# Two PSUM banks for score half tiles and four for the ring, in place of three and three

## The chip, the cores and the metric

One core of a Trainium2 chip (trn2) runs the whole program. The metric is the device time of one execution in microseconds. TensorE (PE in the rows) multiplies, VectorE (DVE) and ScalarE (ACT) read its products from PSUM, GpSimd (POOL) works between SBUF tiles, SyncE (SP) issues most transfers. PSUM has eight banks of 512 fp32 columns, numbered 0 to 7 here.

## The reference, cut to what matters

Two layers of attention over a context of 1601 rows and a feed-forward part, on a batch of 4 with 256 rows of width 512. The change lies in the attention of the second layer, which is grouped: 16 query heads share 4 heads of keys and values.

```python
hidden = jnp.concatenate([context, latents], axis=1)      # 1601 + 256 rows
q = (latents @ Wq.T).reshape(b, q_len, H, HD)             # H = 16, HD = 96
k = (hidden @ Wk.T).reshape(b, s_len, KV, HD)             # KV = 4
v = (hidden @ Wv.T).reshape(b, s_len, KV, HD)
...
scores = jnp.einsum('bkgqd,bksd->bkgqs', q, k) * scale
attn = jax.nn.softmax(scores.astype(jnp.float32), axis=-1).astype(q.dtype)
out = jnp.einsum('bkgqs,bksd->bkgqd', attn, v)
out = out.transpose(...)
return out @ Wo.T
```

After it comes a layer normalisation and a feed-forward part with a small mixture (`L1_ffn`).

## The kernel before, in words

Three functions run one after the other: `context_products` (the context's keys and values), `latent_attention_and_ffn` (the first layer and its feed-forward part), and `grouped_attention` (line 1194 on), the third stage, which takes from about 1012 us to the end. Only that one is touched.

**Segments and tiles.** The stage has S = 16 passes, one for each pair of batch element and key head. They are called segments 0 to 15 here. A segment has 1024 query columns (4 query heads by 256 rows) and 1857 keys in KT = 15 key tiles of 128 (the last of 65). Scores of one tile are 128 keys by 1024 columns, computed as two half tiles of 512 columns, one PSUM bank each. Each half tile of scores is the sum of three matmuls (lines 1502, 1503, 1504), since keys and queries are split in a high and a low part; the column maxima are subtracted through extra rows of the first one.

**What each half tile goes through.** ACT takes the exponential twice (function `probs`): line 1604 writes it rounded to `ph`, line 1607 again in full precision to `pf`. Both read the scores' bank, and it is free when the second is done (semaphore `exp_done`). POOL subtracts them to `pl` (line 1417, `plo`). TensorE then multiplies with the values in three matmuls (lines 1522, 1523, 1525), into two accumulating banks, one for each half, which stay in use for the whole segment. The third waits for POOL. Line 1607 waits for POOL's subtraction of two half tiles ago.

**The ring.** All other products of the stage share a ring of banks: `ring_item` writes product number n into bank `M0 + n % RB`, after DVE has read product n - RB (line 1426). They are, for each segment, 32 products for the maxima of the next segment (line 1435, read by DVE at line 1690), two products of 9 matmuls with the output weights (1458, read at 1698), and in segments 5, 9 and 13 those of the feed-forward part of the batch element that is complete (1466, 1472, 1477, 1480, 1483). `beside(s)` lists the order for TensorE and for DVE alike.

**The order on each engine.** For each tile, TensorE issues the scores of tile kt + 1 (half 0, a ring product, half 1, a ring product) and then the values of tile kt (half 0, a ring product, half 1, a ring product), lines 1542 to 1553; from tile 12 on no ring product stands beside the values. Segment 0 has no ring product for its first tiles, segment 15 none for maxima. At the end of a segment, the maxima are transposed (line 1488, into bank `M0`), and DVE writes them as extra rows (line 96), on which the next segment's first scores wait.

**What stands in ACT's queue besides.** After the exponentials of tile 0 of the next segment, ACT copies the two accumulating banks to `o` (1652) and sends the row sums to eight partitions (1611). Behind tile 2 it waits until DVE has inverted them (1720) and sends them to DRAM (1615); behind tile 3 it waits for that to land and spreads them over 96 partitions (1619); behind tiles 6, 7 and 9 stand the steps that stack the output (1623, 1628, 1635). DVE's inversion stands in its own list after six maxima. In segments 5, 9 and 13 DVE also runs `layernorm` (lines 63 to 88), with a ring product's reading at each `pause` and `between`.

**The banks.** Scores use banks 0 to SB - 1, a half tile with running number i in bank `i % SB`; the accumulators are banks OB and OB + 1; the ring is banks M0 to M0 + RB - 1. TensorE's wait before half tile i of the scores is for `exp_done` of half tile i - SB:

```python
                    if 2 * n + half >= SB:
                        pe.wait_ge(exp_done, 2 * n + half - SB + 1)
                    out = bank((2 * n + half) % SB)[0:m, :]
```

Of the kernel before, what the change touches and what calls it, by code (L numbers as in the profile page):

```python
# [100 lines left out]
def build(nc, A, out):  # L101
# [10 lines left out]
    with ExitStack() as ctx:  # L112
        def sb(name, shape, dt=F32):
            return ctx.enter_context(nc.sbuf_tensor(name, shape, dt))

        ident = sb("ident", [P, P])
        negid = sb("negid", [QT, QT])
        ps = ctx.enter_context(nc.psum_tensor("ps", [P, 8 * BANK], F32))
        ln = {n: sb(f"ln_{n}", s) for n, s in
              (("st", [P, TT, 6]), ("mv", [P, TT, 2]), ("v", [P, TT]), ("t", [P, TT]), ("u", [P, TT]), ("y", [P, TT]))}  # L120
        w1T = sb("w1T", [P, DC, D])
        home = [sb(f"home{i}", [P, n], F32R) for i, n in enumerate((NK + 1, 2 * GC, NK + 1))]
        with ExitStack() as early:
            def weight(name, cols, dt=F32R):
                return early.enter_context(nc.sbuf_tensor(name, [P, DC, cols], dt))

            wkvh, wkvl = weight("wkvh", WV + WK), weight("wkvl", WV + WK)
            wqh, wql = weight("wqh", H1 * HD1), weight("wql", H1 * HD1)
            w0T = weight("w0T", D, F32)
            small = {n: early.enter_context(nc.sbuf_tensor(n, shape, F32)) for n, shape in  # L130
                     (("bias0", [P, D]), ("wqd", [P, DC, LQ]), ("wqk", [LQ, H0, 3 * HD0]), ("wvu", [P, NG * 2, 2, HD0 + 1]),
                      ("cq", [LQ, T]))}
            context_products(nc, A, ident, negid, ps, ln, home, wkvh, wkvl, wqh, wql, w0T, w1T, *small.values(),
                             k_scr, v_scr, cst_scr, cv_scr, wo_scr)
            latent_attention_and_ffn(nc, A, ident, negid, ps, ln, home, wkvh, wkvl, wqh, wql, w0T, *small.values(),
                                     cst_scr, cv_scr, q_scr, k_scr, v_scr, x_scr)
        grouped_attention(nc, A, ident, negid, ps, ln, home, q_scr, k_scr, v_scr, x_scr, wo_scr, sum_scr, o_scr, w1T, out)
# [1056 lines left out]
def grouped_attention(nc, A, ident, negid, ps, ln, home, q_scr, k_scr, v_scr, x_scr, wo_scr, sum_scr, o_scr, w1T, out):  # L1194
# [16 lines left out]
    with ExitStack() as ctx:  # L1211
# [69 lines left out]
        bm_done, zp_done, d_mm, y_done, o_st = sem("bm_scaled"), sem("zp_ready"), sem("delta_product"), sem("y_ready"), \  # L1281
            sem("out_stored")
        block = ctx.enter_context(nc.Block())
        OB, M0, RB, SB = 3, 5, 3, 3

        def bank(i, n=BANK):
            return ps[:, i * BANK:i * BANK + n]
# [550 lines left out]
```

## Time and profile before

| | |
|---|---|
| median of 3 runs | 1970.17 us (1968.33 to 1972.54) |
| the profiled execution | 1970.21 us |
| its span, first to last instruction | 1968.4 us |
| TensorE busy with matmuls | 1880.0 us, 96% of the span |
| DVE, ACT, POOL busy | 1036.9, 906.6, 631.3 us |
| mean granted TensorE clock | 0.966 of full speed |
| third stage | about 1012.7 to 1968.4 us |

Around the span lie 1.8 us of the execution. A row of a timeline gives start and duration in us, the engine, the line, what it wrote and read with the shapes, and in brackets the idle time before it and what ended that. Matmuls are pipelined: one is shown for about 0.4 us, but the next starts 0.23 us after it, so the start of the next one tells more than the duration. PEld is the loading of the weights for a matmul, SPq and ACTq are transfers issued by SP and ACT.

### The profile page before, as it was taken

The page shows a single profiled execution, that of the slowest core. Times are in us where ns is not written, and L with a number is a line of the kernel's source. Part 1 is how long each engine was busy: PE and PEld are TensorE (multiplying, and loading weights), DVE is VectorE, ACT ScalarE, POOL GpSimd, SP SyncE. Part 2 cuts the span into 40 slices and gives each one's busy share as a digit, 9 for nine tenths or more (in the row PEclk, how much of TensorE's full clock was granted, in tenths as well). Part 3 has the DMA queues.
Part 4 walks back from the last instruction along what each step waited for, and adds up shares of the span by engine and source line. Part 5 has one row for each costly group of instructions (what it writes and reads, how often), then busy time and mean ns, then how long its engine had stood idle before and what let it go on. Part 6 is the DMA issues. An engine that isn't in the chain of part 4 may idle for free. (4 is left out here: it accounts for less than half of the span.)

```text
span 1968.4 us, 23187 instructions
## 1 busy us (share of the span) xinstructions
PE 1880.0 (96%) x8570; PEld 1334.5 (68%) x8570; DVE 1036.9 (53%) x1983; ACT 906.6 (46%) x1726; POOL 631.3 (32%) x504
## 2 busy tenths in 40 slices
PE   7999997999999999999899999999999999999997
PEld 6999894444466465555577777767776777767763
DVE  3564435667665665666525444564545455554414
ACT  2333331444344334434236666545655466645650
POOL 0000000000000000000027777757776577765760
PEclk9999995999999999999989999999999999999996
DMA  5978963000111020021177444435544145543101
GB/s 180 287 246 256 291 205 98 0 1 17 43 44 45 16 75 22 33 77 33 54 205 178 121 120 111 111 88 131 133 123 123 51 105 141 131 123 96 53 25 43
DMA packets 192950, 208.42 MB, mean 106 GB/s; under 512 B 87425, under 2 KB 157569, under 8 KB 192838
## 3 DMA queue, kind: packets, MB, share of 16 engines
q1 hardware_dynamic: 177124, 188.92, 33.7%
q10 hardware_dynamic: 15714, 18.03, 3.0%
q8 instruction: 68, 1.11, 0.2%
q14 instruction: 44, 0.36, 0.1%
HBM read 128.90 MB, written 77.94 MB: 105 GB/s over the span
## 5 line engine op out<-in xcount | busy, mean ns | idle before, releaser
L1417 POOL TENSOR_TENSOR pl<-pf,ph 128x512 fp32r<-128x512 f32 (+1 forms) x480 | 623.5, 1321 | 270.9 <-ACT pf L1607 270.3
L1604 ACT ACTIVATE ph<-ps 128x512 fp32r<-128x512 f32 (+1 forms) x480 | 288.1, 600 | 369.8 <-PE ps L1504 309.7
L1690 DVE TENSOR_REDUCE pm<-ps 128x1 f32<-128x464 f32 x480 | 299.8, 636 | 203.0 <-PE ps L1435 199.6
L1140 DVE TENSOR_REDUCE pm<-ps 128x1 f32<-128x400 f32 (+3 forms) x544 | 285.3, 572 | 90.8 <-PE ps L987 86.8
L1047 ACT ACTIVATE pr<-ps 128x512 f32<-128x512 f32 (+1 forms) x416 | 219.6, 600 | 196.0 <-PE ps L919 195.2
L1607 ACT ACTIVATE pf<-ps 128x512 f32<-128x512 f32 (+1 forms) x480 | 289.1, 602 | 3.3 <-POOL pl L1417 2.5
L1406 POOL MEMSET vh<- 128x30 f32 x1 | 0.2, 154 | 700.3 <-POOLq L684 700.3
L932 PE MATMUL ps<-pr,cv 128*64 128x512 f32 (+1 forms) x832 | 210.6, 622 | 0.0
L1522 PE MATMUL ps<-ph,vh 128*97 128x512 f32 (+1 forms) x480 | 191.4, 399 | 0.0
L1525 PE MATMUL ps<-pl,vh 128*97 128x512 f32 (+1 forms) x480 | 190.1, 396 | 1.1 <-POOL pl L1417 0.8
L1523 PE MATMUL ps<-ph,vl 128*97 128x512 f32 (+1 forms) x480 | 189.2, 394 | 0.0
L1435 PE MATMUL ps<-kh,qh 96*128 96x464 f32 x320 | 121.3, 379 | 7.7 <-DVE pm L1690 7.5
L1502 PE MATMUL ps<-qh,kh 104*128 104x512 f32 x300 | 122.2, 407 | 0.1
L932 PEld LDWEIGHTS ps<-pr,cv 128*64 128x64 f32 (+1 forms) x832 | 51.9, 139 | 86.8 <-issue 60.8
L1525 PEld LDWEIGHTS ps<-pl,vh 128*97 128x97 f32 (+1 forms) x480 | 78.0, 163 | 38.7 <-POOL pl L1417 6.2
L901 POOL MEMSET home<- 96x1 f32 x1 | 0.1, 96 | 304.5 <-POOLq L158 304.5
L987 PE MATMUL ps<-home,ast 96*128 96x400 f32 (+1 forms) x256 | 91.6, 420 | 6.1 <-DVE pm L1140 2.6
L1523 PEld LDWEIGHTS ps<-ph,vl 128*97 128x97 f32 (+1 forms) x480 | 78.8, 164 | 26.6
L1522 PEld LDWEIGHTS ps<-ph,vh 128*97 128x97 f32 (+1 forms) x480 | 78.4, 163 | 24.0 <-issue 0.2
L987 PE MATMUL ps<-cst,ast 96*128 96x400 f32 (+1 forms) x256 | 84.3, 386 | 5.7 <-DVE pm L1140 4.1
L987 PEld LDWEIGHTS ps<-home,ast 96*128 96x128 f32 x256 | 49.9, 209 | 57.7 <-DVE pm L1140 28.5
L987 PEld LDWEIGHTS ps<-cst,ast 96*128 96x128 f32 x256 | 45.7, 192 | 54.0 <-DVE pm L1140 33.3
(264 smaller groups left out, 3104.0 us busy)
## 6 DMA issues: line engine op xcount, KB each, us to landing
woT<-wo_turned SPq DMA_DIRECT2D x30, 768.0 KB, 6.0
v_scr<-vst SPq DMA_DIRECT2D x16, 1152.0 KB
cnat<-in_ctx_dram SPq DMA_DIRECT2D x16, 768.0 KB
q_scr<-qst SPq DMA_DIRECT2D x48, 256.0 KB, 2.5
vh<-v_scr SPq DMA_DIRECT2D x15, 672.0 KB
vl<-v_scr SPq DMA_DIRECT2D x15, 672.0 KB
home<-k_scr SPq DMA_DIRECT2D x14, 696.4 KB, 8.4
k_scr<-home SPq DMA_DIRECT2D x24, 384.0 KB, 7.8
```

The costliest lines, as they stand in the source:

```text
L932: mm = pe.matmul(bank(OB)[64 * half:64 * half + 64, :], cv[0:keys[kt], b % 2, kt, :], pr[0:keys[kt], n % NPR, half * BANK:(half + 1) * BAN ...
L987: mm = pe.matmul(out[:, 0:k], queries, keys_t, start=True, stop=True)
L1047: act.activation(pr[0:keys[kt], n % NPR, half * BANK:(half + 1) * BANK], bank((2 * n + half) % SB)[0:keys[kt], :], ACT.Exp, scale=S0).then ...
L1140: dve.reduce_max(pm[:, j, ch:ch + 1], src[:, 0:(cuts if s < S else next_cuts)[ch][1]], AX)\
L1417: pool.tensor_tensor(pl[0:m, n % 2, cols], pf[0:m, half, :], ph[0:m, n % 2, cols].bitcast(F32), ALU.subtract).then_inc(plo, 1)
L1502: pe.matmul(out, kh[s % 3][:, k0:k0 + m], qh[s % 3][:, cols], start=True, stop=False)
L1522: pe.matmul(out, vh[0:m, s % 2, kt, :], ph[0:m, n % 2, cols], start=(kt == 0), stop=False)
L1523: pe.matmul(out, vl[0:m, s % 2, kt, :], ph[0:m, n % 2, cols], start=False, stop=False)
L1525: mm = pe.matmul(out, vh[0:m, s % 2, kt, :], pl[0:m, n % 2, cols], start=False, stop=(kt == KT - 1))
L1604: act.activation(ph[0:keys[kt], n % 2, cols], src, ACT.Exp, scale=S1).then_inc(phi, 1)
L1607: act.activation(pf[0:keys[kt], half, :], src, ACT.Exp, scale=S1).then_inc(exp_done, 1)
L1690: ins = dve.reduce_max(pm[:, j, ch:ch + 1], at[:, 0:cuts[ch][1]], AX)
```

## The change

One line. The ring gets banks 4 to 7 (it had 5 to 7), the scores get banks 0 and 1 (they had 0 to 2), the accumulators move from banks 3 and 4 to banks 2 and 3. All waits follow from the four numbers: that of the scores (line 1499) counts `exp_done` back by two half tiles and not three, that of the ring (line 1426) counts `ring_done` back by four products and not three. ACT's source (line 1601), DVE's source (line 1674), the copies of the accumulators (line 1652) and the bank of the transposed maxima (lines 1488 and 1670) follow too.

```diff
         block = ctx.enter_context(nc.Block())
-        OB, M0, RB, SB = 3, 5, 3, 3
+        OB, M0, RB, SB = 2, 4, 4, 2
```

## Rows read from the trace of the kernel before

**Rows 1.** The page, busy time of each engine (share of the span, instructions)

```profile
PE 1880.0 (96%) x8570; PEld 1334.5 (68%) x8570; DVE 1036.9 (53%) x1983; ACT 906.6 (46%) x1726; POOL 631.3 (32%) x504
```

**Rows 2.** Waits from 890 us on: waiter, releaser, total us, times, longest us

```profile
...
ACT ph L1604 <- DVE sums_inverted L1720: 49.4, 13, 6.6
...
PE ps L1435 <- DVE pm L1690: 11.2, 12, 1.2
...
ACT ph L1604 <- DMA sum_scr<-sums_inverted: 10.2, 5, 2.5
...
```

**Rows 3.** Timeline of segment 2: ACT at tile 4, TensorE at tile 5, half 1

```profile
1133.77 0.32 ACTq L1619 DMA_DIRECT2D o_inverted<-sum_scr  x1
...
1135.64 0.61 ACT L1607 ACTIVATE pf<-ps 128x512 f32<-128x512 f32 x1
...
1135.93 0.40 PE L1502 MATMUL ps<-qh,kh 104*128 104x512 f32 x1
```

**Rows 4.** Timeline of segment 10: the same place, with its two transfers

```profile
1589.15 0.28 ACTq L1615 DMA_DIRECT2D sum_scr<-sums_inverted  x1
...
1593.70 0.32 ACTq L1619 DMA_DIRECT2D o_inverted<-sum_scr  x1
...
1594.62 0.59 ACT L1607 ACTIVATE pf<-ps 128x512 f32<-128x512 f32 x1
...
1595.26 0.50 PE L1502 MATMUL ps<-qh,kh 104*128 104x512 f32 x1
...
1595.58 0.62 ACT L1607 ACTIVATE pf<-ps 128x512 f32<-128x512 f32 x1
...
1595.60 0.40 PE L1503 MATMUL ps<-qh,home 96*128 96x512 f32 x1
...
1595.84 0.39 PE L1504 MATMUL ps<-home,kh 96*128 96x512 f32 x1
...
1597.41 0.40 PE L1523 MATMUL ps<-ph,vl 128*97 128x512 f32 x1
...
1597.88 0.47 PE L1525 MATMUL ps<-pl,vh 128*97 128x512 f32 x1
```

**Rows 5.** Timeline of segment 5: TensorE, DVE and ACT at tiles 2 to 4

```profile
1287.18 0.48 PE L1435 MATMUL ps<-home 96*128 96x464 f32 x1 [1.10 <-DVE pm L1690]
...
1292.59 0.94 DVE L1720 RECIPROCAL sums_inverted<-sums 8x128 f32<-8x128 f32 x1
...
1293.83 2.81 DVE L1690 TENSOR_REDUCE pm<-ps 128x1 f32<-128x464 f32 x5
...
1294.50 0.48 PE L1435 MATMUL ps<-home 96*128 96x464 f32 x1 [1.16 <-DVE pm L1690]
...
1295.40 0.61 ACT L1607 ACTIVATE pf<-ps 128x512 f32<-128x512 f32 x1
...
1296.63 0.40 PE L1502 MATMUL ps<-qh,kh 104*128 104x512 f32 x1
```

**Rows 6.** Start of the stage: timeline, then two windows with PEclk, the granted clock

```profile
1016.46 0.59 ACT L1607 ACTIVATE pf<-ps 128x512 f32<-128x512 f32 x1
...
1017.10 0.79 PE L1502 MATMUL ps<-home 104*128 104x512 f32 x1 [0.21 <-ACT pf L1607]
...
1017.69 0.63 PE L1503 MATMUL ps<-home 96*128 96x512 f32 x1
...
1012.70:1022.10 9.40, 9.18 (x21) 6.43 (x22) 3.90 (x5) 4.22 (x8) 6.32 (x8) 0.50 0.94 213
1022.10:1032.00 9.90, 9.90 (x45) 7.58 (x44) 2.63 (x5) 6.41 (x13) 7.90 (x7) 0.99 1.05 303
```

**Rows 7.** Timeline of segment 15: half 1 of tile 2, and the values behind it

```profile
1866.24 0.61 ACT L1607 ACTIVATE pf<-ps 128x512 f32<-128x512 f32 x1
...
1866.26 0.39 PE L1502 MATMUL ps<-home 104*128 104x512 f32 x1
...
1868.55 0.47 PE L1525 MATMUL ps<-pl,vh 128*97 128x512 f32 x1 [0.28 <-POOL pl L1417]
```

## The prediction, made before the change was run

> **What bounds the kernel now.** I read the page first: TensorE is busy for 1880.0 of 1968.4 us [rows 1], so a time can only come from its few idle stretches, or be lost by new ones. Then the waits of the stage that the change touches. TensorE waits there for DVE's reading of the ring 12 times, 11.2 us in all; this is the only wait that a fourth ring bank can shorten. ACT, which reads the scores, is held for 49.4 us by the inverted row sums and for 10.2 us by their transfer [rows 2]. These ACT stalls reach no TensorE instruction as long as three half tiles of scores are in flight; they are where two banks can be too few. Last, the timeline around each of these places: I call the 16 passes of the stage segments 0 to 15, number the 15 key tiles of each from 0, and ask of each half tile whether the bank that it would now need was free when TensorE got there.
>
> **The two edges of the change.** With three banks, half 0 of tile k waits for the second exponential (L1607) of half 1 of tile k-2; with two it waits for half 0 of tile k-1, and half 1 of tile k for half 1 of tile k-1: one half tile later each. With a fourth ring bank a ring product waits for the fourth last reading instead of the third last. No instruction, transfer or byte is added or removed, and nothing is moved on a queue; SP and POOL issue the same in the same order. So the sum is one of waits alone.
>
> **The price of a wait.** Segment 10 shows the wait that will become usual: the exponential ends at 1594.62 + 0.59 = 1595.21, the product that needs its bank is shown at 1595.26, and the next one starts at 1595.60, where products otherwise follow each other by 0.24 (1595.60 to 1595.84) [rows 4]. So the first one counts as started at 1595.60 - 0.23 = 1595.37, 0.16 after the exponential's end. I use: start = end of the exponential + 0.16, if TensorE is there earlier.
>
> **Tile 5 of the plain segments.** After tile 3 ACT sits behind the transfer of the inverted sums: in segment 2 it issues the next one only at 1133.77, and then computes the four exponentials of tile 4, the last from 1135.64 to 1136.25. TensorE starts half 1 of tile 5 at 1135.93 [rows 3]. With two banks it can start it at 1136.25 + 0.16 = 1136.41: 0.48 late. The DMA, not TensorE, sets ACT's time here, so the delay can't be won back by arriving earlier. The same two rows exist in each of segments 1 to 14. They give 0.48, 0.52, 0.31, 0.08 and 0.14 for segments 2, 3, 7, 8 and 11 (sum 1.53), and nothing for 1, 4 and 14. For segments 6 and 12 they give 0.86. For segment 10 they give 1595.58 + 0.62 + 0.16 = 1596.36 against 1595.37, so 0.99. But in these three TensorE already waits for POOL in the value products of tile 4: in segment 10 from 1597.41 to 1597.88 instead of 0.23 [rows 4]. With the reload behind it (0.08, as in the price above) that is 0.32, and a like wait of 0.2 stands at the other half tile. POOL's time hangs on ACT's and stays. What is left is 0.99 - 0.32 - 0.2 = 0.47 in segment 10 and by the same subtraction 0.36 in segments 6 and 12: together 1.2.
>
> **The ring.** In segments 5, 9 and 13 DVE also computes a layer normalisation. It works without a pause up to the inverse of the sums at 1292.59 and the five maxima from 1293.83, and TensorE waits for it at 1287.18 (1.10), once more between, and at 1294.50 (1.16) [rows 5]. A fourth bank lets TensorE be ahead by one more ring product and the half tile beside it, 0.91 us of its work (three products by 0.23 and one by 0.21); as DVE never pauses between these stalls, that is won once, not three times. So TensorE could come to tile 4 by 0.91 earlier. There it meets the other edge: half 1 of tile 4 now needs the exponential that runs from 1295.40 to 1296.01, so it starts at 1296.17 instead of 1296.63 [rows 5]: a gain of 0.46, not 0.91. The same rows give 0.51 and 0.50 in segments 9 and 13: together 1.5. Nine of the 12 waits, 9.7 of the 11.2 us, are of these segments; the other three, one each in segments 6, 8 and 12, make 1.5 us. They lie just before tile 4, whose scores find their new bank free only 0.0 to 0.1 us before TensorE comes, since ACT and DVE both resume on the same event, the landing of the sums. What a ring bank gives back there is taken by the score bank within 1 us, and I count it at nothing. If this cover is wrong, it is worth up to 1.5 us.
>
> **The start of the stage.** Scores of tile 1 follow at once on those of tile 0. Before, half 1 of tile 1 waits for the first full exponential, which ends at 1016.46 + 0.59 = 1017.05; it is shown at 1017.10 and its successor at 1017.69 [rows 6]. After, half 0 of tile 1 waits for the same one, so everything is later by three products. TensorE's granted clock is 0.50 in this stretch (the lower level, 1.2 GHz), where a product takes about twice as long, 0.43, so 1.28 us are lost; it is 0.99 from 1022.1 on [rows 6], where the same lost work takes half as long to make up. I take 0.64, with 1.3 as the bound if it isn't made up.
>
> **The last segment** has no maxima beside it. Half 1 of tile 2 starts at 1866.26; the bank is now free at 1866.24 + 0.61 + 0.16 = 1867.01, so 0.75 late. At 1868.55 TensorE waits for POOL in any case (0.52 with the reload) [rows 7]. I take 0.23.
>
> **Sum.** 0.64 + 1.53 + 1.2 + 0.23 - 1.5 = +2.1 us. The profiled execution took 1970.21 us, which is the median of the runs (1970.17) to 0.04. Forecast 1970.2 + 2.1 = 1972.3 us, or 0.11% more, which a measurement of this kernel can hardly tell from nothing (it resolves about 0.2%, or 3.9 us). Bounds: the losses are 1.9 if the waits are released at once, and 6.3 if POOL's waits move with them (0.86 + 0.86 + 0.99 + 0.75 in place of 1.4) and the start costs 1.3; the gains are 0 to 4.2. So from -2.3 to +6.3 us.
>
> **Rivals.**
> First, faster: the exponentials are early enough and only the ring counts. Then 0.91 in three segments and 1.5 in the others, 4.2 us, give 1966.0. For it speaks that ACT waits for TensorE, not the reverse, in most tiles. Against it are the ends of the exponentials [rows 3, 4], which lie behind TensorE's present start in eight segments. The Trainium skill goes further: "Perfetto Trace Analysis", section on optimization strategy, says that the same gap repeating on the engine that should be saturated can mean too few buffers for the next tile. By it all 11.2 us of the ring waits [rows 2] would go, and the time would be 1959.0. The rows of DVE without a pause [rows 5] speak against it: there the reader is late, and a buffer only moves the wait. Chances 0.05 for 1966.0 and 0.02 for 1959.0.
> Second, slower: the transfer of the inverted sums lands later in the new order. In segment 10 it took from 1589.15 to 1593.70, 4.55 us [rows 4], the longest of ten such segments, whose mean is 3.7; every 0.1 us on it is 0.1 us on tile 5 as soon as the delay is above zero. If all ten came as late and kept 0.47 each, this term would be 4.7 instead of 2.7 us, and the time 1974.3, slower by 0.21%. The point from which it decides: an average landing of 4.5 us. Where POOL's waits give nothing back either (2.0 us more), it is 1976. Chance 0.18.
> Third, no gain in the normalising segments: something other than the ring holds TensorE there, so that only the losses stand: 1970.2 + 3.6 = 1973.8. Chance 0.12, within the 0.2%.
> Fourth, the banks do nothing: TensorE's order hides both edges, 1970.2. Chance 0.1; the code names the semaphore counts, so this needs the stalls above to cancel.
>
> **How the numbers follow.** The forecast has 0.53, the rivals 0.07, 0.18, 0.12 and 0.1. Faster by more than 0.2%: 0.06, since the first rival lies at the edge. Slower by more than 0.2%: 0.19, from the second rival and a tip of the forecast. The rest, 0.75, is within 0.2%. The range leaves out the ends of the first two rivals: 1967.5 to 1976.5; the runs before alone spread over 4 us.
>
> **What would show it.** Right: TensorE's waits for L1607 in front of L1502 at tile 5 of segments 2, 3, 6, 7, 10 and 12, of 0.1 to 0.8 us each, a longer one at the start of the stage, and some at tile 4; its waits for DVE in front of L1435 down from 11.2 to about 7 us, still in segments 5, 9 and 13; ACT's waits for the sums unchanged. Wrong: no waits for L1607 (then the first rival), waits for L1607 at tiles 8 to 14 (then two banks are too few everywhere, and the loss is several times mine), or ring waits gone altogether.

## The result and the profile after: slower by 0.3%, where 0.1% was forecast

The changed kernel took 1977.24 us in the median (11 runs, 1973.18 to 1983.37) beside 1972.38 us for the kernel before (11 runs, 1964.88 to 1976.51). The ratio is 1.0032 with a 95% interval of 1.0017 to 1.0048: slower, by 3.4 to 9.5 us. A second comparison on another chip gave 1.0042 (1.0029 to 1.0055). The sign of the forecast was right, its size (+2.1 us) was not, and 1977.24 lies above the range. One run of the variant with two score banks and three ring banks, reported below, took 6251.47 us, and that variant's ratio leaves it out.

The page of the profiled execution (1979.45 us, a span of 1977.6), busy times of the engines:

```profile
PE 1891.0 (96%) x8570; PEld 1338.6 (68%) x8570; DVE 1038.5 (53%) x1983; ACT 907.3 (46%) x1726; POOL 631.0 (32%) x504
```

As many matmuls as in [rows 1], but they were busy 11.0 us longer. A matmul behind a wait is shown about 0.1 us longer (0.51 us in the rows below), and TensorE has 13 waits of the two kinds below (for DVE and for L1607) before and after. In a stretch at the lower granted clock every one is shown longer (0.63 us in place of 0.40), and such stretches add up to 156.8 us in this trace, 135.9 in the one before. The waits of the stage (waiter, releaser, total, times, longest), as in [rows 2]:

```profile
ACT ph L1604 <- DVE sums_inverted L1720: 49.3, 13, 6.6
...
ACT ph L1604 <- DMA sum_scr<-sums_inverted: 11.5, 6, 2.5
...
PE ps L1435 <- DVE pm L1690: 5.8, 5, 1.6
...
PE ps L1502 <- ACT pf L1607: 4.1, 8, 1.5
```

ACT's two waits are those of before to 1.3 us. The ring waits fell from 11.2 to 5.8 us, but the longest grew from 1.2 to 1.6, and the wait of the scores for L1607 is there, 1.5 us of it at the start of the stage. Of the other waits of 0.15 us and more in the plain segments, three stand at tile 5 (segments 3, 10 and 12) and three at tile 4 (segments 4, 6 and 8), of which the forecast had said only that there would be some. Tile 5 of segment 2, half 0 and then half 1, the latter being the place of [rows 3]:

```profile
1137.76 0.59 ACT L1607 ACTIVATE pf<-ps 128x512 f32<-128x512 f32 x1
...
1138.40 0.51 PE L1502 MATMUL ps<-qh,kh 104*128 104x512 f32 x1
...
1138.71 0.62 ACT L1607 ACTIVATE pf<-ps 128x512 f32<-128x512 f32 x1
...
1138.75 0.40 PE L1503 MATMUL ps<-qh,home 96*128 96x512 f32 x1
...
1139.38 0.51 PE L1502 MATMUL ps<-qh,kh 104*128 104x512 f32 x1
1139.73 0.40 PE L1503 MATMUL ps<-qh,home 96*128 96x512 f32 x1
```

For half 0 the exponential ends at 1138.35, the product is shown at 1138.40 and its successor at 1138.75, so it counts as started at 1138.52: 0.17 after the end, where the price was 0.16. For half 1 the exponential ends at 1139.33 and the product counts as started at 1139.50, again 0.17 after. TensorE thus meets the delay first at half 0, and half 1 follows its own exponential as forecast.

What the forecast lacked stands in segment 9, where DVE normalises. TensorE in the timeline:

```profile
1528.32 0.48 PE L1435 MATMUL ps<-kh,qh 96*128 96x466 f32 x1 [1.63 <-DVE pm L1690]
...
1529.45 0.76 PE L1435 MATMUL ps<-kh,qh 96*128 96x464 f32 x1
1530.01 0.63 PE L1522 MATMUL ps<-ph,vh 128*97 128x512 f32 x1
1530.43 0.63 PE L1523 MATMUL ps<-ph,vl 128*97 128x512 f32 x1
1530.86 0.63 PE L1525 MATMUL ps<-pl,vh 128*97 128x512 f32 x1
```

After one idle of 1.63 us, which ended at 1528.32, the products follow each other by 0.43 us instead of 0.23. The windows around it (busy us and count of each engine, then PEclk, the granted clock, DMA share and GB/s), and those of the same segment in the kernel before:

```profile
1519.90:1529.40 9.50, 7.87 (x34) 5.66 (x32) 9.01 (x20) 4.29 (x9) 5.83 (x5) 1.00 1.14 255
1529.40:1532.80 3.40, 3.40 (x9) 2.19 (x8) 3.26 (x8) 0.43 (x1) 0.00 (x0) 0.50 0.24 50
1532.80:1542.00 9.20, 9.10 (x43) 6.83 (x43) 7.76 (x13) 5.92 (x12) 7.35 (x6) 1.00 0.15 43
```

```profile
1511.00:1520.50 9.50, 7.23 (x31) 5.06 (x31) 8.14 (x17) 5.22 (x11) 6.74 (x6) 1.00 1.12 234
1520.50:1530.50 10.00, 8.82 (x38) 6.23 (x39) 8.54 (x19) 4.13 (x8) 4.71 (x4) 1.00 0.41 103
```

The granted clock fell to 0.50, the lower of its two levels (1.2 GHz), for 3.4 us. Before, TensorE was busy for less of the stretch (7.23 of 9.5 us against 7.87), with pauses of 1.11 and 1.16 us in it and a third of 1.18 us behind it, and kept the full clock. The same fall is in segment 13 for 3.4 us, and in segment 5 for 10.2:

```profile
1297.30:1307.50 10.20, 9.89 (x24) 6.43 (x23) 6.78 (x12) 4.25 (x8) 5.07 (x4) 0.50 0.13 44
```

From the starts of the first score products, the segments of the two profiled executions compare as follows (us, after minus before): segment 0 +0.6; the ten plain ones +3.3; the normalising ones 5, 9 and 13 +2.6, -0.5 and +1.1; segments 14 and 15 +0.2 together, up to the last value product; what follows it was 0.4 shorter. The stage began 2.2 us later, though nothing ahead of it was changed: low stretches of the clock in the first two stages fall differently from run to run (85.3 and 92.2 us in all in the two traces of the kernel before, 88.7 and 92.2 in those of the changed one).

### The profile page after: what moved, and what is told of

Its sections match the earlier page's. It is cut to its first block and busy times, and to the rows that moved or that the text cites. A ratio compares the mean times of both kernels' runs of the same rounds, so it can differ in the third digit from the quotient of the medians.

```text
span 1977.6 us, 23187 instructions
## 1 busy us (share of the span) xinstructions
PE 1891.0 (96%) x8570; PEld 1338.6 (68%) x8570; DVE 1038.5 (53%) x1983; ACT 907.3 (46%) x1726; POOL 631.0 (32%) x504
## 3 DMA queue, kind: packets, MB, share of 16 engines
q8 instruction: 68, 1.11, 0.2%
## 5 line engine op out<-in xcount | busy, mean ns | idle before, releaser
L1607 ACT ACTIVATE pf<-ps 128x512 f32<-128x512 f32 (+1 forms) x480 | 289.8, 604 | 0.3 <-POOL pl L1417 0.3
L1502 PE MATMUL ps<-home 104*128 104x512 f32 x180 | 75.7, 421 | 7.6 <-PEq L684 4.6
```

What stands on the lines that cost most here:

```text
L1502: pe.matmul(out, kh[s % 3][:, k0:k0 + m], qh[s % 3][:, cols], start=True, stop=False)
L1607: act.activation(pf[0:keys[kt], half, :], src, ACT.Exp, scale=S1).then_inc(exp_done, 1)
```

## The experiments

Three theories were set against each other. **A**: the fourth ring bank makes fewer and longer waits of TensorE's waits for DVE in the normalising segments, and the clock falls. **B**: the clock falls there by chance in any kernel, and the loss is that of the score waits and transfers. **C**: the two score banks bring the clock down. The first four runs shared a chip, the last four another; "before" in each line is the kernel before on that chip (1970.47 and 1971.97 us).

**The kernel before, again** (no edit).

> The kernel before, unchanged. It tells how far its own runs and traces spread. Three theories are at stake. A: the fourth ring bank turns the three short waits of TensorE for DVE in each of segments 5, 9 and 13 into fewer, longer ones, and TensorE's granted clock falls there; that is what my forecast lacked. B: the clock falls at such places in any run of any of these kernels by chance, and the changed kernel's trace merely caught more of it; the loss is that of the score waits and of late transfers. C: the clock falls because of the two score banks. By A and C the trace of this kernel shows no or one low stretch of the granted clock in segments 1 to 15, by B two or three. Time within 0.15% of the kernel before.

Measured: 1971.69 us, ratio 1.0005 (0.9994 to 1.0016). In the trace no low stretch stands inside segments 1 to 15, and segments 5, 9 and 13 took 68.66, 68.89 and 68.66 us (68.63, 68.92 and 68.65 in the first trace). They are the same to 0.03 us where the clock is the same, so a difference of 1 us there is not chance. The ten plain segments took 533.4 us in place of 535.8, since they hang on when the sums land: one trace is good to 2 us on that term. B is weakened.

**The changed kernel, again** (no edit).

> The changed kernel, unchanged. By A and C again two or three low stretches of the granted clock in segments 5, 9 and 13, and 5 to 7 us above the kernel before. By B the number of them differs from the first trace (none or one), and where they are fewer the third stage is 3 to 4 us longer than before and not 7.

Measured: 1978.43 us, ratio 1.0042 (1.0029 to 1.0055). Again a low stretch in each of segments 5, 9 and 13, 3.4 us each, and 69.64, 69.89 and 69.69 us for them. The ring waits there were 1.3 to 1.6 us and 1.2 us, and each fall began 1.2 to 1.5 us after the second. Six falls in six such segments of this kernel, none in six of the kernel before. For segment 5:

```profile
1301.90:1305.30 3.40, 3.40 (x10) 2.55 (x9) 2.20 (x4) 2.46 (x5) 3.15 (x4) 0.50 0.36 116
```

**Two score banks, three ring banks.**

```diff
-        OB, M0, RB, SB = 2, 4, 4, 2
+        OB, M0, RB, SB = 2, 4, 3, 2
```

> Two banks for scores, but the ring keeps three (one bank is unused). By A: no low stretches in segments 5, 9 and 13, ring waits there as in the kernel before (about 9.7 us), score waits at the start, at tile 5 and in segment 15 as forecast, 3 to 4 us above before (0.15 to 0.2%). By C: low stretches as in the changed kernel and 6 to 8 us above before. By B: 3 to 4 us with low stretches in some segments.

Measured: 1974.90 us, ratio 1.0019 (1.0009 to 1.0030), 3.7 us by the ratio. Waits of TensorE in the stage:

```profile
PE ps L1435 <- DVE pm L1690: 10.9, 12, 1.2
...
PE ps L1502 <- ACT pf L1607: 3.0, 5, 1.5
```

No low stretch in segments 5, 9 and 13, which took 68.62, 68.90 and 68.66 us as before; segment 0 lost 0.64 us, segment 15 lost 0.22. C falls. The score banks alone cost what the forecast's losses add up to (3.6 us). The rest of the slowdown comes with the fourth ring bank, the half of the change that was to shorten a wait: 1.0042 against 1.0019 on one chip. These two intervals just touch (1.0029 and 1.0030); the segments of the traces are what separates them, 206.2 us for the three normalising ones here and 209.2 in the changed kernel.

**The changed kernel with the normalisation cut finer.** DVE reads one more ring product at each of five new places.

```diff
+    more()
     chain.link(dve.tensor_scalar(y[:, :].bitcast(I32), t[:, :].bitcast(I32), -1.0, RSQRT_GUESS, ALU.mult, ALU.add))
...
         chain.link(dve.tensor_tensor(t[:, :], y[:, :], y[:, :], ALU.mult))
+        if it < 2:
+            more()
         chain.link(dve.scalar_tensor_tensor(u[:, :], t[:, :], -0.5, v[:, :], ALU.mult, ALU.mult))
+        if it < 2:
+            more()
```

> The changed kernel with the layer normalisation of segments 5, 9 and 13 cut at five more places, at each of which DVE reads one ring product first. DVE then falls behind by less at a time. By A: the waits for DVE in front of L1435 in these segments shrink to under 3 us in all, no low stretches there, and the time is 5 to 9 us below the changed kernel's, thus at or below the kernel before. By B the time falls by the waits alone (3 to 6 us) and low stretches are still seen. By C the low stretches stay.

Measured: 1975.60 us, ratio 1.0028 (1.0017 to 1.0040), 2.8 us below the changed kernel beside it: less than expected. Its waits (five lines lower in this source: L1440 is the ring, L1471 the turning of the normalised rows):

```profile
PE ps L1507 <- ACT pf L1612: 4.4, 11, 1.1
PE ps L1471 <- DVE xn L90: 4.3, 3, 1.8
PE ps L1440 <- DVE pm L1695: 3.1, 6, 0.7
```

The ring waits did fall to 3.1 us, but the normalisation now ends later and TensorE waits for its result, once in each of the three segments. In segment 13 the clock fell (3.4 us) with this wait; in segments 5 and 9 it didn't. A had expected no fall at all. The three segments took 205.8 us in place of 209.2. But the waits moved to another place, so this run tells little about A.

**The changed kernel with the old depth in three segments.** All banks as changed, but there TensorE waits as if the ring had three.

```diff
+                deep = RB - 1 if kind == "max" and a in (6, 10, 14) else RB
                 if n >= RB:
-                    pe.wait_ge(ring_done, n - RB + 1)
+                    pe.wait_ge(ring_done, n - deep + 1)
```

> The changed kernel, with all its banks, but in segments 5, 9 and 13 TensorE waits before a maxima product for the third last reading instead of the fourth last, as before the change; elsewhere for the fourth last. By A (the pattern of waits, not the banks, brings the clock down) there is no low stretch of the granted clock in segments 5, 9 and 13, these segments take 68.6 to 68.9 us each as in the kernel before, and the kernel lies 3 to 4 us above before, where the one with two score banks and three ring banks lies, and some 4 us below the changed one. By the rival that the place of the banks matters (accumulators in banks 2 and 3, ring in 4 to 7), the low stretches stay and the time is that of the changed kernel.

Measured: 1976.26 us, ratio 1.0020 (1.0009 to 1.0030), 3.9 us by the ratio and within the 3 to 4 expected. TensorE in segment 5, from the timeline:

```profile
1292.53 0.48 PE L1436 MATMUL ps<-home 96*128 96x464 f32 x1 [1.10 <-DVE pm L1691]
...
1295.24 0.48 PE L1436 MATMUL ps<-home 96*128 96x464 f32 x1 [0.84 <-DVE pm L1691]
...
1299.86 0.48 PE L1436 MATMUL ps<-home 96*128 96x464 f32 x1 [1.16 <-DVE pm L1691]
```

and two windows over these waits and behind them:

```profile
1290.00:1300.00 10.00, 6.90 (x27) 4.03 (x26) 9.52 (x23) 2.92 (x7) 4.29 (x4) 1.00 0.88 188
1300.00:1310.00 10.00, 10.00 (x49) 7.93 (x50) 7.90 (x13) 6.03 (x12) 8.00 (x6) 1.00 0.11 39
```

The three waits are back with the lengths of before, 9.7 us over the three segments, the clock stays at 1.00, and the segments take 68.63, 68.90 and 68.67 us. With more waiting for the ring these segments are 3.0 to 3.2 us shorter in all than in the two traces of the changed kernel. The whole time agrees (1.0020 against 1.0032 and 1.0042), though the three were not measured on one chip and the intervals overlap or touch. This is theory A, and the rival that the place of the banks matters falls: the banks are those of the changed kernel, only the pattern of the waits is not.

**The changed kernel with the sums later.** DVE inverts the sums after nine maxima instead of six and multiplies with them after 16 instead of 14; four of ACT's five steps stand one tile later.

```diff
-            order = most[:6] + own[:1] + most[6:14] + later[:2] + own[1:2] + most[14:19] + ...
+            order = most[:9] + own[:1] + most[9:14] + later[:2] + most[14:16] + own[1:2] + most[16:19] + ...
...
-                        step = {2: send_parts, 3: spread_parts, 6: send_o, 7: stack_o, 9: stacked_hi}.get(kt)
+                        step = {3: send_parts, 4: spread_parts, 7: send_o, 8: stack_o, 9: stacked_hi}.get(kt)
```

> The changed kernel, with the inversion of the sums after nine maxima instead of six, and ACT's five steps behind tiles 3, 4, 7, 8 and 9 instead of 2, 3, 6, 7 and 9. ACT then doesn't sit behind a transfer while tiles 3 to 5 wait for it. My theory of the plain segments (the score wait at tile 5 comes from ACT's late exponentials) expects no waits for L1607 at tile 5 and plain segments of 53.0 us (about 0.8 us less each than in the changed kernel, 8 us over ten of them). Rival: two banks are too few in any tile, then waits for L1607 are spread over the tiles and the plain segments stay above 53.4 us. Segments 5, 9 and 13 keep ring waits, and by A low stretches: in all 5 to 9 us below the changed kernel.

Measured: 1964.53 us, ratio 0.9961 (0.9948 to 0.9973). The waits from 1020 to 1900 us:

```profile
ACT ph L1604 <- PE ps L1504: 362.1, 243, 4.8
...
PE ps L1435 <- DVE pm L1690: 5.5, 6, 1.8
...
PE ps L1502 <- ACT pf L1607: 0.2, 1, 0.2
```

ACT no longer waits for the sums, and TensorE's wait for L1607 behind the start is 0.2 us. The ten plain segments took from 52.95 to 53.13 us, 530.3 in all, where the two traces of the changed kernel have 539.1 and 539.7. So two score banks are enough in every tile but those that stand behind ACT's stalls (and at the start and in the last segment), as the forecast held. The normalising segments kept one long wait of 1.5 to 1.8 us each and low stretches of 3.4, 6.8 and 6.8 us, as A expects. In segment 9:

```profile
1514.70:1521.50 6.80, 6.51 (x16) 4.88 (x17) 6.56 (x15) 2.17 (x4) 2.55 (x2) 0.50 0.44 95
```

**Both edits on the banks of before, and on the changed ones.** The finer normalisation, the later sums (a little later still), and the turned rows behind 17 maxima instead of 14, so that they aren't waited for.

```diff
-            order = most[:6] + own[:1] + most[6:14] + later[:2] + own[1:2] + most[14:19] + later[2:3] + most[19:23] + ...
+            order = most[:9] + own[:1] + most[9:17] + later[:2] + most[17:18] + own[1:2] + most[18:20] + later[2:3] + most[20:23] + ...
```

> The banks of before (three and three), with the sums later as in the run above, the layer normalisation cut at five more places, and its turned products two places later in the order. Expected: plain segments at 53.0 us, ring waits in segments 5, 9 and 13 down from 9.7 to under 3 us, no low stretches; 10 to 16 us below the kernel before (ratio 0.992 to 0.995). If DVE is the limit in these segments whatever the order, 4 to 6 us below.

Measured: 1964.15 us, ratio 0.9959 (0.9946 to 0.9971). Plain segments at 53.0 to 53.1 us, no low stretch in the normalising ones, which took 67.76, 67.97 and 67.74. The wait for the ring came down to 5.1 us only:

```profile
PE ps L1440 <- DVE pm L1695: 5.1, 7, 1.3
```

A gain of 8 us where 10 to 16 were expected. The ring waits fell only from 9.7 to 5.1 us, where under 3 were expected, and the three segments became 2.7 us shorter in all; the ten plain ones became 4.2 us shorter than the mean of the two traces before.

> The same edits on the changed kernel's banks (two and four). With both sources of waits gone the division of the banks shouldn't matter but at the start of the stage (0.6 us): within 0.1% of the run above. If two score banks cost something of their own in every tile, it is over 3 us slower than the run above; if the fourth ring bank is worth something once nothing else holds TensorE, 1 to 3 us faster.

Measured: 1961.65 us, ratio 0.9946 (0.9932 to 0.9959), the fastest of all and 0.5% below the kernel before. Its waits in the stage:

```profile
PE ps L1440 <- DVE pm L1695: 3.8, 6, 1.0
...
PE ps L1507 <- ACT pf L1612: 0.2, 1, 0.2
```

The longest ring wait is 1.0 us, there is no low stretch, and segments 5, 9 and 13 took 66.75, 66.67 and 66.72 us: 3.3 us less in all than with three ring banks in the run above, for 0.5 us lost in segment 0. By the traces the stage is 3.0 us shorter with the changed banks once the stalls around them are gone; the ratios of the two runs overlap, so the medians alone would not show it.

## Why the prediction was right in sign and wrong in size

**The base.** The forecast of 1972.3 us is +2.1 on a base of 1970.2, the median of three runs; with eleven runs that median is 1972.38. So of the 4.9 us by which 1977.24 lies above the forecast, 2.2 are the base, and 1977.24 would have been inside the range without them. Against the kernel before, the change cost 4.9 us by the medians and 6.3 by the ratio, and 8.3 by the ratio of the second comparison, which is above the bound of +6.3 that I had worked out. The size of the change was wrong in both.

**The price of a score wait** held: 0.17 against 0.16 us. **The start** held: 0.64 us forecast, 0.64 and 0.66 in the two variants without the clock's falls, 0.6 and 1.1 in the traces of the changed kernel. **The last segment** held: 0.23 forecast, 0.20 and 0.24 in the traces of the changed kernel, against the mean of the two before.

**Tile 5 of the plain segments** was the right mechanism, shown by the run with the later sums. The term was +2.7 us (1.53 + 1.2). The means of two traces each give +4.8 (539.4 against 534.6 us over ten segments). Of the 2.1 us missed, 1.2 lie in the base: the one trace that I read had slow transfers in segments 6 and 12, and so longer ring waits to set the loss against; the second has 2.4 us less. The other 0.9 I can only place in part. The rows give 0.96 and 0.97 us for segments 6 and 12, not the 0.86 that I took, which is 0.2 in all. Waits at tile 4, which I had set to nothing against the ring's gain, are 0.9 and 1.8 us in the two traces, where the ring waits that they replace were 1.5 and 0.4. And single transfers landed late, such as 4.1 us in segment 3 where I had read 3.7. How much each of these gave isn't shown. That every 0.1 us of landing counts stood in the second rival; its mean rose by 0.1 us (3.75 and 3.65 us against 3.69 and 3.54) and not to 4.5, so that rival isn't what happened.

**The normalising segments** are the step that failed. I wrote that the fourth bank lets TensorE be ahead by one more product and that "as DVE never pauses between these stalls, that is won once, not three times", so 1.5 us are gained. (Three products by 0.23 and one by 0.21 are 0.90 and not 0.91, and three by 0.43 at the start 1.29 and not 1.28; nothing hangs on either.) TensorE does win something: segment 9 of the first trace is 0.5 us shorter in spite of 3.4 us at the lower clock. But I worked with the length of the waits alone and left out what they do together. Before, a segment has three waits of 0.8 to 1.2 us. Being one product further ahead, TensorE doesn't stop for the first of them and meets DVE later in one pause of 1.3 to 1.6 us, with the last wait of 1.2 us behind it in four of the six segments traced; and in each of the six the granted clock falls to 0.50 for 3.4 to 10.2 us, 1.1 to 1.8 us after the last of these waits of over 1 us. In place of -1.5 us the three segments gave +3.2 and +3.0 us in the two traces: 4.6 us of the 7.2 and 8.4 us by which these executions (1979.45 and 1980.73) exceed the forecast. No rival had it: I had weighed the clock only at the start of the stage, where it is low anyway.

**The rivals.** The first (faster, 1966.0) and its extreme (1959.0) fell. By the Trainium skill, "Perfetto Trace Analysis", section on optimization strategy, a repeating gap can mean too few buffers; here one more buffer took the ring waits from 11.2 to 5.8 and 7.9 us and the time went up. The measurement decides: the gap's cause was a late reader, as DVE's unbroken row in [rows 5] had said. The third rival (1973.8) was right that the normalising segments give no gain, for another reason: its 3.6 us of losses are what the variant with two score banks and three ring banks cost. Nearest in time was the tip of the second (1976), whose condition wasn't met. The fourth (nothing happens) fell with the wait rows.

That the pattern of the waits brings the clock down is shown by the variant with the old depth. What stays open is by which rule, and why the low stretch is 3.4 us in one segment and 10.2 in another. The clock fell in all nine normalising segments whose longest ring wait was 1.31 to 1.79 us (both traces of the changed kernel, and that with the sums later), and in none of the 18 in which it was 0.95 to 1.30 us (six traces). The two groups all but touch. And in the run with the finer cut TensorE waited 1.66, 0.80 and 1.80 us for the turned rows, and only the last was followed by a fall. So length alone is not the rule.

## What to carry to other kernels

Before a buffer is added against a repeating wait, look whether the reader pauses between the waits: if it doesn't, the buffer only moves and merges them, and on TensorE one longer pause can cost more than several short ones did, through the clock. Where a queue of exponentials also carries steps that wait for a transfer, place them where the transfer has landed by then; here this took 9 us off the ten plain segments of the changed kernel and 4 off those on the banks of before, and they then take 530.5 us on the banks of before and 530.4 on the changed ones. A buffer can pay once its reader is no longer late: in the last two runs the fourth ring bank, which costs time in the changed kernel, made the normalising segments 3.3 us shorter. And a term read from one trace carries that trace's luck with transfers: read the same stretch in two before a difference of 2 us is forecast.

## What the runs showed of the hardware that I had not expected

TensorE's granted clock fell to its lower level after a single idle of 1.63 us in a stretch that was 7.87 of 9.5 us busy, and stayed at the full level over a stretch that was 6.90 of 10.0 us busy, with pauses of 1.10, 0.84 and 1.16 us. Segments in which neither the clock nor a transfer plays in repeat from run to run to 0.04 us (68.63, 68.66, 68.62, 68.63 for segment 5 in four traces), while the whole program spreads over some 10 us. Much of that goes with the clock: of the eleven runs of the changed kernel the fastest (1973.18 us) had a mean granted clock of 0.964, the slowest (1983.37 us) one of 0.958.
